# Five narrow rows of key products go to TensorE as two f16 halves instead of one f32 matrix

## The reference

```
x = x + 0.5 * ffn(layernorm(x))
x = x + attn(layernorm(x))       # attn itself: y + scan_out @ w_out + b_out
x = x + 0.5 * ffn(layernorm(x))
ffn(y):  h = silu(y w1) * (y w2);  h = gelu(h h1);  h = gelu(h h2);  h w3   # 256 -> 1024 -> 1024 -> 1024 -> 256
attn(y): q, k, v, beta of 16 heads with 16 features; k is normalised per head; then per token t
    S = S + (beta_t * (v_t - S k_t)) k_t^T
    o_t = S q_t
```

## Time and profile before

| | |
|---|---|
| median of 3 runs | 1817.02 us (1816.15 to 1817.09) |
| the profiled execution, its time and its span | 1815.88 us, 1814.2 us |
| granted clock of PE, mean | 0.995 |
| PE busy | 1730.7 us (95%) |
| PEld busy | 1068.7 us (59%) |
| DVE busy | 1243.6 us (69%) |
| POOL busy | 1209.4 us (67%) |
| ACT busy | 1057.8 us (58%) |
| DMA | 7 tenths in the first slice of 40, 1 in the second, then none |

### The profile page before, as it was taken

One profiled execution on the slowest core, in us unless ns is written; L12 is line 12 of the kernel. 1 busy time (PEld: TensorE's weight loads), 2 busy tenths in 40 slices (PEclk: granted clock), 3 DMA queues, 4 the chain that ended last, 5 costly groups with the idle time before them and its releaser, 6 DMA issues.

```text
span 1814.2 us, 29738 instructions
## 1 busy us (share of the span) xinstructions
PE 1730.7 (95%) x10030; PEld 1068.7 (59%) x10030; DVE 1243.6 (69%) x2890; ACT 1057.8 (58%) x2115; POOL 1209.4 (67%) x1501
## 2 busy tenths in 40 slices
PE   6989989999999999999999999999999999999999
PEld 5855545555555555555555555588655555555588
DVE  5255776777776877868767687777776768777331
ACT  4656565465656565656556474667656565655454
POOL 4463876767676767777676667677776767675653
PEclk9999999999999999999999999999999999999999
DMA  7100000000000000000000000000000000000000
GB/s 290 43 1 1 1 1 1 1 1 2 0 2 0 24 1 24 1 1 1 1 1 1 1 24 1 1 25 1 1 1 1 1 1 13 1 1 12 1 13 13
DMA packets 5270, 23.16 MB, mean 13 GB/s; under 512 B 640, under 2 KB 1664, under 8 KB 3584
## 3 DMA queue, kind: packets, MB, share of 16 engines
q1 hardware_dynamic: 5120, 21.26, 3.2%
HBM read 17.06 MB, written 4.19 MB: 12 GB/s over the span
## 4 chain that ended last, share of the span: by engine, by line
PE 66%; DVE 9%; issue 8%; POOL 8%; ACT 7%; POOLq 0%; DVEq 0%; ACTq 0%
PE ffn_bank L1073 39%; PE ffn_bank L1056 7%; PE att_bank L1121 5%; PE att_bank L1093 4%; POOL hid_lo L565 3%; PE state_bank L1129 2%; PE att_bank L1108 2%; POOL pairs_lo L602 2%; PE ln_bank L1024 2%; PE att_bank L1109 2%; POOL pairs L594 2%; ACT hid L680 2%; DVE hid L821 1%; ACT L680 1%; PE att_bank L1138 1%
## 5 line engine op out<-in xcount | busy, mean ns | idle before, releaser
L1073 PE MATMUL ffn_bank<-hid_hi,w_sb 128*128 128x512 f16 (+1 forms) x2736 | 904.6, 346 | 7.8 <-ACT gate L667 4.6
L1073 PE MATMUL ffn_bank<-hid_lo,w_sb 128*128 128x512 f16 (+1 forms) x2736 | 904.3, 346 | 0.0
L565 POOL TENSOR_TENSOR hid_lo<-hid,hid_hi 128x512 f16<-128x512 f32 (+1 forms) x456 | 463.3, 1032 | 294.8 <-ACT hid_hi L656 294.5
L594 POOL TENSOR_TENSOR pairs<-KQ 128x32 f32<-128x32 f32 (+15 forms) x496 | 326.5, 669 | 122.8 <-DVE KQ L848 104.5
L1073 PEld LDWEIGHTS ffn_bank<-hid_hi,w_sb 128*128 128x128 fp8e4 x2736 | 275.6, 101 | 206.3 <-issue 11.5
L1073 PEld LDWEIGHTS ffn_bank<-hid_lo,w_sb 128*128 128x128 fp8e4 x2736 | 268.2, 98 | 205.4 <-issue 12.7
L602 POOL TENSOR_TENSOR pairs_lo<-pairs,pairs_hi 128x448 f16<-128x448 f32 (+15 forms) x416 | 313.4, 758 | 75.7 <-ACT pairs_hi L728 75.4
L728 ACT CAST pairs_hi<-pairs 128x448 f16<-128x448 f32 (+15 forms) x416 | 175.2, 440 | 158.6 <-POOL pairs L594 157.3
L656 ACT CAST hid_hi<-hid 128x512 f16<-128x512 f32 (+1 forms) x456 | 235.4, 553 | 30.1 <-DVE hid L821 29.4
L680 ACT ACTIVATE hid<-ffn_bank,par_sb 128x512 f32<-128x512 f32 (+1 forms) x304 | 172.1, 617 | 123.1 <-PE ffn_bank L1073 122.4
L1056 PE MATMUL ffn_bank<-xn_hi,w_sb 128*128 128x512 f16 (+1 forms) x608 | 204.7, 351 | 16.3 <-DVE w_sb L770 6.3
(11 more groups left out here) (88 smaller groups left out, 2103.2 us busy)
## 6 DMA issues: line engine op xcount, KB each, us to landing
NK<-in_w SPq DMA_DIRECT2D x11, 1024.0 KB, 5.9
X<-in_x SPq DMA_DIRECT2D x7, 512.0 KB, 3.6
out<-X SPq DMA_DIRECT2D x7, 512.0 KB, 2.6
wqkvb_sb<-in_wqkvb SPq DMA_DIRECT2D x1, 1024.0 KB, 8.4
X<-in_x SPq DMA_DIRECT2D x2, 256.0 KB, 6.4
out<-X SPq DMA_DIRECT2D x2, 256.0 KB, 2.1
wout_sb<-in_wout SPq DMA_DIRECT2D x1, 256.0 KB, 9.2
par_sb<-in_par SPq DMA_DIRECT2D x1, 24.0 KB, 2.4
```

What stands on the lines that cost most here:

```text
L565: pool.tensor_tensor(hid_lo[layer % 2][:, m, call.cols], hid[:, u % HID_BUFFERS, call.cols], hid_hi[layer % 2][:, m, call.cols], ALU.subtr ...
L594: pool.tensor_tensor(packed(pair(pairs, q, dot), n), later, earlier, ALU.mult).then_inc(pairs_made if dot in SPLIT else pairs_ready, 1)
L1073: mm = nc.tensor.matmul(ffn_ps(call, j), weight(name, kk, 2 * pair + i), v[:, kk, cols], start=kk == 0 and part == 0, stop=kk == KT_FF - 1 ...
```

## The change

One number: `SPLIT_FROM["kk"]` goes from 6 to 1.

```diff
-SPLIT_FROM = {"kk": 6, "qk": 0}
+SPLIT_FROM = {"kk": 1, "qk": 0}
 SPLIT = {use: q for q, use in enumerate(u for u in DOTS if u[2] >= SPLIT_FROM[u[0]])}
```

## The result

The changed kernel takes 1823.1 us (median of 5 runs, 1821.29 to 1824.6) where the kernel before takes 1816.15 (5 runs). The ratio is 1.0037, 95% interval 1.0026 to 1.0049: slower by 4.7 to 8.9 us. A second session gave 1823.87 us and 1.0041 (1.0028 to 1.0054). The forecast was 1818.5 us, no measurable change (within 3.6 us), range 1810 to 1825. The kernel became slower instead, to which the prediction gave 0.28. The time lies in the range, at rival (b): PE's gain is there, POOL's subtraction becomes PE's wait, and nothing comes back.

What follows compares the result with a forecast made beforehand. PE, busy 95% of the span, was taken as the bound. 1815.9 - 8.4 (PE) + 11.0 (lateness) - 2.8 (recovery) + 1.7 (clock) = 1817.4 us profiled, 1818.5 us for the median; range 1810 to 1825 us.

Steps and rivals of the forecast that it cites:

- rival (b): At the row of 128 columns, POOL's subtraction becomes PE's wait, nothing comes back: 1823.0 us, chance 0.25.
- PE's gain, 8.4 us: Five narrow rows as f16 pairs instead of f32 save PE 0.53 us per half, 16 halves.
- The loss at the narrow rows, 11.0 us: POOL's added subtraction comes late for PE, mostly at the row of 128 columns, in some halves: 11.0 us.
- I take a quarter of the 11.0 us back, 2.8 us: Behind the narrow rows, engines behind PE catch up while it stands, shortening later waits by 2.8 us.
- The sign that the prediction had named for this: All of PE's waits together growing by over 15 us would show the recovery wrong.
- The clock, 1.7 us: One drop of PE's granted clock behind a new wait of 2.8 us costs 1.7 us, bounds 0 and 5.1.
- (a): Lateness at the narrow rows falls into waits PE had anyway, so its gain comes through: 1812.3 us, chance 0.27.
- (c): The f16 pair on PE saves nothing, leaving only the change's costs: 1826.9 us, chance 0.03.
- the lower bound, 0: Least that POOL's freed 18.3 us of buffer waits could give back to PE's waits for L602; upper bound 20.7 us.

Runs made afterwards that it cites:

- PE's part alone: Kernel before, with the five narrow k.k rows as two f16 matmuls on PE, no added cast or subtraction: 1807.33 us, ratio 0.9958.
- The steps alone: Changed kernel's casts, subtractions and order, but PE takes the five narrow rows as f32 products: 1828.87 us, ratio 1.0074 to the kernel before.
- the steps early: Changed kernel, with cast and subtraction of the 128 and 160 column rows 8 and 7 ticks ahead instead of 4 and 3: 1806.8 us, ratio 0.9952.
- rows 6 and 7 early: Kernel before, with the already split rows of 192 and 224 columns made 11, cast 8, subtracted 7 ticks ahead: 1808.79 us, ratio 0.9958.
- t = 4 and 5 only: Changed kernel, but of the five narrow rows only 128 and 160 columns are split, the others stay f32: 1825.06 us, ratio 1.004.

## Why the prediction was right in its range and low in its value

- **PE's gain, 8.4 us: right.** PE's part alone gave 7.6 (5.3 to 10). The trace after has the two matmuls of 128 columns 0.06 us apart (218.62 and 218.68). By the sustained roofline of the Trainium skill ("TensorE: Matmul & The Clock Gate", "Back-to-back issue gap"), about 81 ns for a matmul of 128 columns, the gain was estimated at 3.5 us. The trace and the run don't agree with that.
- **The loss at the narrow rows, 11.0 us, at the row of 128 behind two `hid_lo`: right in place, a little low in size.** The steps alone cost 13.4 us (11 to 16), clock included, against 11.0 + 1.7 = 12.7. PE's wait for L602 grew by 15.9 us where some 10 were named, 12 net of the waits for whole products. Two smaller signs were off: ACT's busy time grew by 14 us and not 22, since some of its records overlap, and PE's fell to 1725.9 us and not to 1722.
- **"I take a quarter of the 11.0 us back, 2.8 us": this is the step that failed.** Nothing came back. The delay of 3.43 us behind the fourth half was 3.40 a frame later, and no stretch between the narrow rows took any back except where a drop of the clock was missing. I had argued that engines behind PE catch up while it stands. PE's other waits were as long as before even so. The likely reason is that they are for work that PE itself releases, a few microseconds before, so that DVE and ACT start later by as much as PE does. I haven't followed each of these chains. The sign that the prediction had named for this, all of PE's waits together up by over 15 us, did not show: they grew by 13.5 us. It was set too high.
- **The clock, 1.7 us: the right kind, too small.** Of three new waits of 2.60, 2.61 and 3.46 us in the second, fourth and tenth half, two were followed by a drop in the profiled execution, 1.7 us each, and the same two in the second one. The rest of the difference in mean clock (0.992 against 0.995) is at places that the change doesn't touch, and varies between executions.
- With no recovery and two drops, the prediction's own sum is 1817.0 - 8.4 + 11.0 + 3.4 = 1823.0 us; measured 1823.1. That was rival (b), at 0.25. (a) fell, and so did (c). That the two agree to 0.1 us is luck: 1817.0 was the median of three runs where five gave 1816.15, so the change cost 7.0 us by the medians and the sum has 6.0.
- POOL's 18.3 us of waiting for PE went, and nothing shows that it bought anything: PE's old waits at 192 columns are as long as before. That is the lower bound, 0.

## What to carry to other kernels

When a change makes a cheap instruction wait for one step more, price the step by what stands ahead of it in its queue, not by its own 0.4 us: here the place was worth 16 us, clock included, and the work nothing that could be measured (1806.8 us with the steps early, 1807.33 with no steps at all). Work out the lateness instance by instance, and count none of it as given back later unless you can name the wait that would shrink. And when a form change is meant to help, run it with the schedule fitted to it (here two rows' steps four ticks earlier) before it is judged, and run the kernel before with an order improved in the same way too: here that (rows 6 and 7 early) reached nearly the same time.

## What the runs showed of the hardware

PE waits of about 2.6 us were followed by a drop of the granted clock to the lower level in some places and not in others. Behind the one of 2.60 us at 218.62 the clock was 1.00 (218.3 to 224 us), and behind the one of 2.61 us at 419.47 it dropped. With t = 4 and 5 only, there was a drop in the second half as well (0.72 from 216 to 222 us), behind a wait of 2.06 us. The drops read here cost 1.7 us of full speed each, but for the one in the tenth half, 3.4 us in the second execution. So the time of one and the same program spread over 11 us (1818.95 to 1830.07, t = 4 and 5 only), the longest runs with the lowest mean clock.
